# Cross-attention and FFN on one core: seven max tiles with one transpose, softmax sums over pairs of key tiles added on GpSimd, and no loop

## The reference

```python
x = x + xattn(layernorm(x), ctx, ctx)      # 16 heads of 32; q, k, v and output projections with biases
x = x + ffn(layernorm(x))                  # 512 -> 1408 -> 512, activations and weights through blockwise FP4

scores = einsum('bhqd,bhkd->bhqk', qh, kh) / sqrt(32)
attn   = softmax(scores, axis=-1)
out    = einsum('bhqk,bhkd->bhqd', attn, vh)
# fp4_quant_dequant: blocks of 16, scale = max(|x|)/6, round to the grid 0 .5 1 1.5 2 3 4 6
h = silu(fp4_linear(x, w_gate)) * fp4_linear(x, w_up);  y = fp4_linear(h, w_down)
```

## Time and profile before

| | us |
|---|---|
| median of 3 runs | 2333.55 (2331.75 to 2346.21) |
| the profiled execution | 2336.36 |
| its span, first to last instruction | 2334.6 |

### The profile page before, as it was taken

One profiled execution on the slowest core, in us unless ns is written; L12 is line 12 of the kernel. 1 busy time (PEld: TensorE's weight loads), 2 busy tenths in 40 slices (PEclk: granted clock), 3 DMA queues, 4 the chain that ended last, 5 costly groups with the idle time before them and its releaser, 6 DMA issues. The chain is left out here.

```text
span 2334.6 us, 50290 instructions
## 1 busy us (share of the span) xinstructions
PE 2207.3 (95%) x17444; PEld 1867.7 (80%) x17444; DVE 1797.0 (77%) x3107; ACT 845.4 (36%) x1677; POOL 198.4 (9%) x226
## 2 busy tenths in 40 slices
PE   5999999999999999999999999975999999999998
PEld 4888888888888888888888788843788888888886
DVE  4777777777777676776777777747999999999986
ACT  4444444454444444444445444433111111111111
POOL 1011111110101111011111010100000000000000
PEclk9999999999999999999999999987999999999999
DMA  5343434434344344343443434324010100100100
GB/s 159 101 115 90 125 85 120 119 88 124 101 104 119 85 118 118 87 121 88 112 121 88 122 85 120 94 75 152 19 37 27 40 27 27 40 27 27 36 19 28
DMA packets 124062, 197.78 MB, mean 85 GB/s; under 512 B 29776, under 2 KB 72272, under 8 KB 121280
## 3 DMA queue, kind: packets, MB, share of 16 engines
q1 hardware_dynamic: 123840, 194.86, 30.1%
HBM read 75.67 MB, written 23.33 MB: 42 GB/s over the span
## 5 line engine op out<-in xcount | busy, mean ns | idle before, releaser
L612 DVE TENSOR_REDUCE row_max<-max_bank 112x1 f32<-112x376 f32 (+1 forms) x1024 | 523.0, 541 | 328.9 <-PE max_bank L471 324.1
L537 ACT ACTIVATE probs<-score_bank 125x448 f32<-125x448 f32 x768 | 405.2, 543 | 310.4 <-PE score_bank L486 302.6
L471 PE MATMUL max_bank<-k_high,q_masked 128*112 128x376 f32 (+1 forms) x1024 | 313.6, 352 | 22.5 <-DVE row_max L612 18.3
L486 PE MATMUL score_bank<-qstack,kstack 100*128 100x224 f32 x1536 | 301.9, 282 | 16.3 <-issue 12.5
L486 PEld LDWEIGHTS score_bank<-qstack,kstack 100*128 100x128 f32 x1536 | 263.6, 191 | 46.6 <-issue 40.0
L1146 ACT ACTIVATE f_act_gate<-gate_bank 128x512 f32<-128x512 f32 (+1 forms) x84 | 47.3, 563 | 516.7 <-PE up_bank L1101 516.7
L501 PE MATMUL pv_bank<-probs,values 125*32 125x224 f32 x3072 | 223.7, 363 | 9.3 <-ACT probs L537 9.3
L1101 PE MATMUL gate_bank<-ffn_gate_hi,f_xqt 128*128 128x512 f32 (+1 forms) x672 | 218.9, 387 | 8.1 <-DVE f_xqt L1207 8.1
L445 PE MATMUL proj_bank<-wv_hi,ctx_hi 128*128 128x256 f32 x768 | 221.1, 288 | 4.3 <-DVE wo_lo L691 4.3
L507 PE MATMUL pv_bank<-probs,ones 125*32 125x224 f32 x3072 | 218.9, 357 | 0.0
L471 PEld LDWEIGHTS max_bank<-k_high,q_masked 128*112 128x112 f32 x1024 | 161.6, 177 | 69.2 <-DVE row_max L612 37.7
(11 more groups left out here) (121 smaller groups left out, 4164.8 us busy)
## 6 DMA issues: line engine op xcount, KB each, us to landing
kstack<-k_high SPq DMA_DIRECT2D x512, 93.8 KB, 2.2
ctx_raw<-in_ctx SPq DMA_DIRECT2D x16, 1500.0 KB, 7.3
kstack<-k_low SPq DMA_DIRECT2D x256, 93.8 KB, 2.2
qstack<-q_part SPq DMA_DIRECT2D x768, 28.0 KB, 1.9
ffn_quant<-fw_share SPq DMA_DIRECT2D x48, 176.0 KB, 1.9
fw_raw<-ffn_quant SPq DMA_DIRECT2D x33, 256.0 KB, 4.0
xn<-in_x SPq DMA_DIRECT2D x16, 448.0 KB, 8.1
res<-in_x SPq DMA_DIRECT2D x16, 448.0 KB, 3.8
```

The lines of the kernel that those rows point to most:

```text
L471: nc.tensor.matmul(out[0:QH, 0:hi - lo], q_masked[t % 2][:, j, half * QH:(half + 1) * QH], k_part[t % 2][0][:, lo:hi], start=True, stop=Tr ...
L486: last = nc.tensor.matmul(score_bank[j % 2][:, k * SQ:(k + 1) * SQ], kstack[t % 2][0:STK, j, kt * KW:kt * KW + P], qstack[t % 2][:, j, :], ...
L537: nc.scalar.activation(probs[p][:, j, :, :], score_bank[j % 2][0:KW, 0:2 * SQ].rearrange("p (k q) -> p k q", k=2), ACT.Exp, scale=float(DK ...
L612: nc.vector.tensor_reduce(row_max[:, half, j, kh:kh + 1], mbank[0:QH, 0:KSPLIT[kh + 1] - KSPLIT[kh]], AX.X, ALU.max).then_inc(max_reduced, 1)
```

## The change

1. **Max in seven tiles.** The 4 x 224 = 896 masked query columns are taken as 7 tiles of 128 (`MT = HG*SQ // P`) without regard to heads: 14 matmuls of 128 columns and 14 reductions per slot in place of 16 and 16. One small reduction gives all negated maxima, one 128 x 128 transpose turns them, and VectorE (not ScalarE) writes the shift rows: one product of the seven transposed rows, spread, with an identity, 7 x 896 elements. The stacked operands have 103 rows in place of 100, and the stacked k holds ones where the 4 x 4 identity was.
2. **Sums over pairs.** GpSimd adds the two key tiles of a pair (unit "pair", 125 x 896, three per slot) into `pair_sum[p]`, and TensorE multiplies only the three pair sums with the ones (unit "sum"): 12 matmuls per slot in place of 24. "sum" waits for the pair, the exp of the next group waits for the pair too, and the pair waits for the "sum" of the group before. "inverse" waits for the last "sum".
3. **Places.** One new table of places for every unit in every slot. "pv" and "sum" share places, and some lie at 12 or more, that is, in the next slot.
4. **No loop.** Batches 1 to 14 are written out, so that all waits have constant values.

```diff
+MT = HG * SQ // P
-STK = SHIFT + HG
+STK = SHIFT + MT
 # PLACES and SLOT_PLACES become one PLACES of four slots; of slot 0:
-        "max": (0.15, 0.15, 0.74, 1.46, 1.97, 2.82, 3.42, 4.78, 4.89, 5.54, 6.68, 6.73, 7.87, 7.94, 8.54, 9.17),
-        "shift": (5.97, 10.64),
-        "pv": (6.66, 11.9),
-        "pv_last": 0.15,
-        "q": 7.12,
-        "ffn_quant": (3.25, 4.97, 6.08, 6.45, 7.12, 8.21, 8.35, 9.18, 9.62, 10.0, 10.54),
+        "max": (0.05, 0.23, 0.69, 1.42, 1.72, 1.93, 2.58, 3.68, 4.07, 6.41, 7.36, 7.93, 8.71, 8.8),
+        "shift": 11.35,
+        "pv": (8.62, 12.45, 12.45),
+        "pair": (2.62, 6.92, 7.57),
+        "q": 7.37,
+        "ffn_quant": (2.22, 3.11, 3.45, 4.76, 5.78, 8.2, 8.49, 9.49, 10.07, 11.9, 11.9),
 # of slots 1, 2 and 3:
+        "pv": (12.05, 14.53, 15.0),
+        "pair": (0.86, 5.95, 9.14),
+        "pv": (8.55, 12.62, 13.8),
+        "pair": (4.14, 4.29, 12.12),
+        "pv": (10.7, 12.62, 13.05),
+        "pair": (2.43, 4.25, 11.65),
+def attend_units(g):
+    at = PLACES[g % NG]
+    return [(place, (kind, g, p)) for kind, places in (("pair", "pair"), ("pv", "pv"), ("sum", "pv")) for p, place in enumerate(at[places])]
-        with engine.Fori(0, (batches - 2) // 2) as i:
-            body(2 * i + 1, batch_units(False, False), list(v_end), list(m_end))
-            body(2 * i + 2, batch_units(False, False), list(v_end), list(m_end))
+        for b in range(1, batches - 1):
+            body(b, batch_units(False, False), list(v_end), list(m_end))
 # TensorE
-                    half, j, kh = u[2] // 8, u[2] % 8 // 2, u[2] % 2
+                    m, kh = u[2] // 2, u[2] % 2
-                    nc.tensor.matmul(out[0:QH, 0:hi - lo], q_masked[t % 2][:, j, half * QH:(half + 1) * QH],
+                    nc.tensor.matmul(out[:, 0:hi - lo], masked_columns[t % 2][:, m * P:(m + 1) * P],
-                    nc.tensor.transpose(out[:, 0:QH], neg_max[:, u[2], :],
-                                        ident[0:QH, 0:QH]).then_inc(made["shift"], 1)
+                    nc.tensor.transpose(out[:, 0:P], neg_max[:, :], ident[:, :]).then_inc(made["shift"], 1)
-
-                        for j in range(HG):
-                            last = nc.tensor.matmul(pv_bank[t % 2][j * DK:(j + 1) * DK, SQ:2 * SQ], ones[0:KW, :],
-                                                    probs[p][:, j, k, :], start=False, stop=(kt == KT - 1),
-                                                    skip_group_check=True)
                     last.then_inc(made["pv"], 1)
+                elif kind == "sum":
+                    p = u[2]
+                    reached(pe, paired, count(b, *u))
+                    for j in range(HG):
+                        last = nc.tensor.matmul(pv_bank[t % 2][j * DK:(j + 1) * DK, SQ:2 * SQ], ones[0:KW, :],
+                                                pair_sum[p][:, j, :], start=False, stop=(p == 2),
+                                                skip_group_check=True)
+                    last.then_inc(made["sum"], 1)
 # ScalarE
                         reached(act, made["pv"], count(b, "pv", t - 1, p))
+                        reached(act, paired, count(b, "sum", t - 1, p))
-                elif kind == "shift":
-                    act.wait_ge(made["shift"], count(b, *u))
-                    row = mbank[SHIFT:STK, 0:QH].unsqueeze(1).to_broadcast([HG, HG, QH])
-                    nc.scalar.activation(qstack[t % 2][SHIFT:STK, :, u[2] * QH:(u[2] + 1) * QH], row,
-                                         ACT.Copy).then_inc(shift_copied, 1)
 # VectorE
-                    nc.vector.tensor_reduce(row_max[:, half, j, kh:kh + 1], mbank[0:QH, 0:KSPLIT[kh + 1] - KSPLIT[kh]],
+                    nc.vector.tensor_reduce(row_max[:, m, kh:kh + 1], mbank[:, 0:KSPLIT[kh + 1] - KSPLIT[kh]],
+                elif kind == "shift":
+                    dve.wait_ge(made["shift"], count(b, *u))
+                    reached(dve, made["score"], count(b, "score", t - 2, 2, 3))
+                    nc.vector.tensor_tensor(shift_rows[t % 2][SHIFT:STK, :, :],
+                                            mbank[SHIFT:STK, 0:P].unsqueeze(1).to_broadcast([MT, MT, P]),
+                                            ident[SHIFT:STK, SHIFT:STK].unsqueeze(2).to_broadcast([MT, MT, P]),
+                                            ALU.mult).then_inc(shift_copied, 1)
                     reached(dve, made["pv"], count(b, "pv", t, 2))
+                    reached(dve, made["sum"], count(b, "sum", t, 2))
 # GpSimd
+                if kind == "pair":
+                    p = u[2]
+                    pool.wait_ge(exp_done, count(b, "score", t, p, HG - 1))
+                    reached(pool, made["sum"], count(b, "sum", t - 1, p))
+                    nc.gpsimd.tensor_tensor(pair_sum[p][:, :, :], probs[p][:, :, 0, :],
+                                            probs[p][:, :, 1, :], ALU.add).then_inc(paired, 1)
```

More of the change, by code:

```diff
@@ L96 @@
     {
[L97 to L116, removed]
+        "max": (0.05, 0.39, 0.51, 0.54, 1.81, 3.24, 4.51, 4.83, 5.26, 6.88, 9.14, 9.3, 9.86, 10.5),
+        "shift": 11.9,
+        "pv": (12.05, 14.53, 15.0),
+        "pair": (0.86, 5.95, 9.14),
+        "inverse": (1.25, 3.95),
+        "heads": 4.36,
+        "heads_hi": 6.32,
+        "sum_lo": 11.65,
+        "k": (1.18, 4.78),
+        "k_lo": (3.04, 4.9),
+        "q": 8.18,
+        "q_lo": 9.68,
+        "v": (9.63, 11.85, 11.9),
+        "out": (3.29, 6.66),
+        "ctx": (0.05, 0.75, 2.71, 4.13),
+        "xt": (1.85, 8.39),
+        "xt_lo": (6.06, 9.06),
+        "norm": (4.53, 7.65),
+        "norm2": (10.98, 11.9),
         "load": 2.6,
         "load_res": 6.6,
-        "ffn_quant": (3.81, 4.25, 4.6, 4.7, 5.64, 7.25, 8.05, 8.99, 9.45, 11.45, 11.51),
+        "add_bias": 11.9,
+        "ffn_quant": (1.66, 1.73, 2.79, 4.71, 5.95, 6.51, 6.92, 8.55, 9.84, 11.9, 11.9),
         "ffn_store": 11.6,
@@ L122 @@
     {
[L123 to L141, removed]
[L142 removed]
+        "max": (0.05, 0.05, 0.2, 0.28, 1.7, 3.13, 5.24, 5.52, 5.95, 6.44, 7.11, 8.26, 8.71, 11.21),
+        "shift": 11.9,
+        "pv": (8.55, 12.62, 13.8),
+        "pair": (4.14, 4.29, 12.12),
+        "inverse": (5.02, 10.57),
+        "heads": 11.37,
+        "heads_hi": 11.9,
+        "sum_lo": 11.9,
+        "k": (5.42, 5.99),
+        "k_lo": (6.4, 7.16),
+        "q": 7.72,
+        "q_lo": 9.88,
+        "v": (10.96, 11.35, 11.9),
+        "out": (10.47, 11.9),
+        "ctx": (0.42, 0.73, 2.03, 2.99),
+        "xt": (0.05, 4.04),
+        "xt_lo": (0.25, 5.39),
+        "norm": (0.05, 5.92),
+        "norm2": (8.42, 11.69),
         "load": 2.6,
         "load_res": 6.6,
[L145 removed]
+        "add_bias": 11.9,
+        "ffn_quant": (2.25, 4.45, 6.21, 9.06, 9.82, 10.04, 10.26, 10.71, 10.73, 10.73, 11.9),
         "ffn_store": 11.6,
@@ L188, in add @@
         placed.extend(zip(places, units))
+    placed += [(place, unit) for place, unit in attend_units(g) if place < 12]
+    if not (first and g == 0):
+        placed += [(place - 12, unit) for place, unit in attend_units(g - 1) if place >= 12]
     ahead = not (last and g == NG - 1)
@@ L313, in attention @@
     pv_bank = [bank(f"pv_bank{i}") for i in range(2)]
-    names = ("score", "max", "shift", "k", "q", "v", "xt", "out", "pv")
+    names = ("score", "max", "shift", "k", "q", "v", "xt", "out", "pv", "sum")
     made = {n: sem(f"{n}_made") for n in names}
@@ L359, in index_of @@
             return ((b + unit[1]) * 2 + unit[2]) * KT + unit[3]
-        per = {"score": 12, "max": 16, "shift": 2, "k": 2, "q": 1, "pv": 3, "sum": 1}
+        per = {"score": 12, "max": 2 * MT, "shift": 1, "k": 2, "q": 1, "pv": 3, "sum": 3, "normalized": 1}
         if kind in per:
@@ L441, in body @@
                     half, kt = u[2], u[3]
+                    if half == 0 and kt == 0:
+                        reached(pe, lo_done["ctx"], count(b, "ctx", t, KC - 1))
                     n = 0
```

152 lines of the change are left out of this document (72 added, 80 removed).

## The result

The changed kernel takes 2351.24 us (median of 4 runs, 2349.83 to 2352.34), the kernel before 2334.74 us beside it: a ratio of 1.0062 (95% interval 1.0039 to 1.0086). It is slower by 0.6%, a small change but one clear of the noise, where 2219 us was forecast. 132 us of expected gain are missing.

The account below looks back on a forecast made before the run. TensorE was taken to bound the attention, so its savings count almost fully: 2334.6 - 73.0 (ones) - 23.0 (max) - 4.5 (transposes) - 15 (loop) + 0.5 = 2219.6 us of span, forecast 2219 us, range 2172 to 2268.

Parts of the forecast that it names:

- TensorE's side: Attention matmuls: ones groups halved save 73.0 us, max matmuls 16 to 14 save 23.0, one transpose per slot 4.5.
- the jump: Loop's jump back, where TensorE waits for its own issue: writing out the batches was taken to save 15 us.
- the amount of the holds: VectorE instructions held by GpSimd in the attention: 14 us per batch, VectorE then busy 81 of 87 us.
- rival 3: Pair addition bare in TensorE's path, 2.1 us per slot, 134 us in all, whole 2353 us; chance 0.04.
- rival 4: Ones groups no cheaper or sums cost extra switches: 21 to 69 us taken back, up to 2288 us; chance 0.05.
- zero net: Extra holds in TensorE's way and waits removed by the new places taken as equal, from -40 to +60 us.
- a good part of the quantization stands behind the last max unit of the slot: New places, slot 0 from 9.49 and slot 3 from 10.08: a held instruction there delays no reduction.
- rival 1: VectorE becomes late through holds by GpSimd: a batch 91 us, +60 us, whole 2279 us; chance 0.19.
- several us to spare: GpSimd's queue behind the pairs: masked q, layernorm's powers and bias addition each have several us before they are needed.
- -1.24 + 1.10, nothing within 10 us: VectorE per slot loses three reductions (1.24 us), gains the shift product (1.10): no change within 10 us for 64 slots.
- no gain: ScalarE loses the transposes' two copies; since it is busy under half of the time, nothing is saved.
- SP's queue gets nothing new: DMA queue of SP: the change adds nothing to it, and no cost was counted.

Follow-up runs that it names:

- experiment 10: Changed kernel with pair additions cut to one column, slot 1's first four quantization steps later, and the shift product cut to one block of seven: 2206.60 us, 0.9455.
- experiment 1: Changed kernel with each GpSimd pair addition cut to one column of 224, true softmax sums left out: 2289.57 us, 0.9805.
- experiment 9: Changed kernel with VectorE's shift product cut to one block of seven, the other shifts left zero: 2307.01 us, 0.9874.
- experiment 11: Changed kernel without pair additions, ones matmuls over all six key tiles, slot 1's first four quantization steps later, all work done: 2279.65 us, 0.9756.
- experiment 2: Changed kernel with the first four quantization steps of slot 1 moved to later places: 2323.97 us, 0.9948.
- experiments 6 and 7: Changed kernel with residual load and bias additions in slot 2, 2434.83 us; then also quantization steps and slot 1's "sum_lo" moved, 2388.07 us.

## Why the prediction was wrong

**What held.** TensorE's side did: the ones groups halve, the max matmuls fall to 14, a max matmul of 128 columns still costs 0.17 us from start to start (446.66 to 446.83), the jump was worth 13.6 us for 15, and experiment 10 comes to 2207 us for 2219 once nothing else stands in the way. The unseen durations did too: the shift product 1.097 us for 1.10, the pair addition 2.125 us in the median (2.233 in the mean) for 2.1. Even the amount of the holds did: VectorE was to be busy 81 us per batch and was 79 to 80. Of the 9 us more than before in batch 4, experiment 1 gives 7.0 to the pairs; I put the rest down to other holds in the new order, which no run separates. TensorE's waits for GpSimd's pairs themselves were 0.5 us in all, as forecast (rival 3 did not occur; nor rival 4).

**The step that failed first: "zero net" for the holds.** I had the 14 us per batch and then set them against the waits that the new places might remove, because "a good part of the quantization stands behind the last max unit of the slot". That is just where they cost: behind the last max unit of a slot come the shift product and the first reductions of the next one, on the same queue. The pair additions were worth 62 us (experiment 1). That rival 1 has +60 is luck: it came from a batch of 91 us, and the batch is 95. The two bias additions, which the prediction gave "several us to spare", follow the last pair without a gap; I read their cost as GpSimd's latency and did not see that three steps of VectorE beside them would take 4.65 us in place of 1.4.

**The second: "-1.24 + 1.10, nothing within 10 us".** The two reductions that went were spread over the slot, in time that VectorE had to spare. The product that came stands at the end of a chain, last reduction, transpose, product, first score. An exchange of equal durations was an exchange of slack for path. Cutting the product by 0.80 us gave back 44 us beside the pairs (experiment 9), and by the estimate from experiment 11 it costs about nothing without them; what the two lost reductions gave back no run shows. Before, ScalarE did each of its two copies in 0.54 us with half of its time free; "no gain" for its relief was right, and a loss for moving it was not looked for.

**The third: "SP's queue gets nothing new".** True of the DMAs' number, but the places moved the end of slot 0's chain to 11.9 and the start of slot 1's to 1.66, and a store and a load through SP's queue lie between (6.6 us). 27 us (experiment 2), and up to 81 us of VectorE's waiting when slot 0 is quick (experiment 1).

**A term that was absent.** After a stall of 2.3 us at the start of slot 0 the granted clock shows 0.93 for the slot. In experiment 1 slot 0 has 1.00 again and slot 1, where TensorE then stands, has 0.94; in experiment 10 all four slots have 1.00. Some 1.7 us per batch lie in the clock; no run separates them from the stall.

The right mechanism stood among the rivals at 0.19, but rival 1 was priced alone, for 2279 us; that three delays on one engine's queue, each in front of the next slot's start, would make each other dearer was in no case. What stays open is whether an order exists in which the pairs on GpSimd pay. Experiment 10's 2207 us are reached with the pair additions all but left out, and experiments 6 and 7 show only that mine did not find such an order.

## What to carry to other kernels

On an engine that is 75% busy, work is not free by its share: ask for each added or moved instruction which chain it ends, and what is queued behind it there. If an addition goes to GpSimd, the VectorE instructions with two SBUF operands, and the fast one-operand ones, that start beside it last until it ends and 0.2 to 0.4 us more; put them where no chain passes, above all not at the seam between two slots. And when a unit is moved to the end of a slot and its successor to the start of the next, what lies between them on the DMA queue is now bare.

## What the runs showed of the hardware

A VectorE instruction that starts during a GpSimd instruction and is held ends a fixed time behind it: 0.20 us for L871 (one operand; 32 cases, 199 to 202 ns), 0.38 us for L869, L873 and L874 (two operands in SBUF; 60 cases, 379 to 388 ns). Mostly this is so also when the next GpSimd instruction follows at once: L873 and L874 took 1.49 and 1.47 us beside two bias additions that follow each other. In the kernel before, though, one L850 that began 25 ns before a bias addition's end lasted through the next, 1.65 us.

The holding goes both ways. Of the 192 pair additions 79 met none of VectorE's "ctx", "sum_lo" and "norm2" steps nor a 352-column quantization step other than its reduction; they took 2.10 to 2.13 us. The 15 that started during a "ctx" step with two SBUF operands (L656, 0.93 us) took 2.80 to 2.83, and those that started during one of the fast one-operand steps L864 and L871 up to 2.29. The Trainium skill (Advanced Engine Details and Errata, section VectorE Performance Modes) says that GpSimd and two-port VectorE instructions block each other; the trace agrees for both directions with the fast one-operand steps (L871: 0.34 us free, 1.69 beside a pair addition), and shows the same for two-operand instructions. Reductions and products with an operand in PSUM kept their time beside GpSimd: L614's median is 0.536 us in the 298 of its 896 runs that a pair, mask or bias addition overlaps and 0.540 in the others, and the shift product took 1.096 to 1.098 us in all 64 cases, though 15 pair additions started during it.
